# One chunk projected ahead of the gate's loop, row splits in two buffers, one late set of scatters, projections without loops

## The chip, the cores and the metric

One core of a Trainium2 chip runs one whole decoder layer as one program. The metric is the time of one execution on the device in microseconds (us).

## The reference

The input is x (4 x 1024 tokens of 512 floats) and a context (4 x 2048 tokens). Everything is float32; the kernel gets that precision on TensorE by splitting each operand into a rounded high part and the rest, and by adding three products (hi·hi, hi·lo, lo·hi).

```
x = x + self_attention(norm(x))            # causal, 16 heads of 32; q, k, v, out: y @ W.T
x = x + cross_attention(norm(x), context)  # 16 heads; Q, K, V: y @ W; out @ W_o + b_o
h = norm(x)
scores = h @ gate_W + gate_b               # 4 experts
top two experts of each token, softmax over the two scores
expert e: norm(relu(norm(h @ W1 + b1) * g1 + be1) @ W2 + b2) * g2 + be2
x = x + h + sum over the two of weight * expert(h)
```

## The kernel before, in words

The program is a row of stages with a barrier of all engines between them: constants, the projection of x to q, k and v (`project`, called as "qkv1"), the self attention, a "bridge" (output projection, norm, cross queries), the projection of the context ("kv2", `project` again, with weights that the bridge has split), the cross attention, `finish`, and `experts`. Each engine has its own list of instructions, in an order written out by hand, and waits on semaphores. SP's queue issues the loads and stores, strictly in its order, and a wait there holds everything behind it.

`project` works in chunks of 512 tokens (4 tiles of 128). A tile is turned on TensorE (L359), split by ScalarE (high, L327) and VectorE (low, L282); the next chunk's tiles are turned between the 12 products of this one (L376, L379). Each product is 12 matmuls. For qkv1 a block of its own, `load_weights` (L75), comes first: it turns and splits each of the three 512 x 512 matrices whole, in one PSUM buffer. Then a second block starts the norm (L261 to L276) and the products. The first three batches are passes of a hardware loop (L195), the last is written out.

`finish` goes over 8 chunks of 512 tokens. For chunk c it loads the attention rows (`a_in`, two buffers, L1345), splits them (`a_hi`, `a_lo`, one buffer each, L1453 and L1516), projects them tile by tile (`project_tile`, 14 matmuls, L1634 to L1637) and adds them to the tokens in `x_in` (three buffers, L1522). Then come the moments (L1495), a root on GpSimd (L1389), the normalising on ScalarE (L1439 and, for the output's base, L1443), stores of both (L1372, L1374), the turn (L1643) and split (L1469, L1600), the gate's scores (L1663), their turn (L1671) and the gate on VectorE (L1532 to L1553). Eight tiles (chunks 0 and 1) are projected before the loop; in turn c of the loop chunk c+2 is projected between the turns of chunk c. A chunk's tokens may be loaded once the base that lay in their buffer is stored:

```python
def load(c):
    after(sp, base_stored[c % 3], 16 * (c // 3))
```

In turn c SP issues, in this order: attention rows of c+3, `xn` of c, base of c, tokens of c+3, and in every second turn a matrix of the experts' first weights (`raw`, two buffers, L1355), which ScalarE and VectorE split (L1448, L1512).

The gate puts each token into the list of its two experts, in DRAM, by indirect DMAs of GpSimd, here called scatters: 16 for a chunk, 128 entries of 8 bytes each (L1397). Chunks 0 to 5 are scattered in `finish`, each set in the turn behind its gate and behind that turn's root. The last `LATE` = 2 chunks' 32 scatters are the first work of GpSimd in `experts` (L1821); SP loads the lists when all have landed (L1790), GpSimd gathers the tokens (L1798), TensorE turns them (L1849), they are split (L1900, L1965), and the first product begins (L1839). Meanwhile the second weights are loaded and split (L1895, L1989), in the lists of ScalarE and VectorE ahead of the first tokens.

## Time and profile before

| | |
|---|---|
| median of 3 runs | 4392.72 us (4384.69 to 4401.05) |
| profiled execution | 4395.31 us, its span 4393.6 us |
| TensorE busy | 4007.7 us, 91% of the span |
| VectorE, GpSimd, ScalarE busy | 62%, 59%, 48% |
| first product | 50.43 us |
| finish begins, experts' first scatter, first product | 3563.33, 3828.40, 3894.78 us |

A share over the whole span says little about stages that differ; the rows below are of the stages that the change touches. "Idle before" in a row is the time in which that engine did nothing ahead of the instruction, and the arrow names what ended it.

### The profile page before, as it was taken

What the parts mean: (1) busy time and instruction counts of PE and PEld (TensorE: products, weight loads), DVE (VectorE), ACT (ScalarE), POOL (GpSimd) and SP (SyncE); (2) the same over time, 40 slices, a digit from 0 to 9 for tenths busy, and PEclk for the clock granted to TensorE, in tenths of its full rate; (3) what the DMA queues carried; (4) which work ended last, traced back from release to release, by engine and by line L of the source; (5) the groups of instructions that cost most, each with busy time, mean ns of one, the idle gap of its engine ahead of it and who ended that gap; (6) DMA issues with size and microseconds to landing.
All of it is one profiled execution on the core that took longest, in us unless ns stands there. A gap on an engine that the chain in (4) does not pass through costs nothing. (4 is left out here: it accounts for less than half of the span.)

```text
span 4393.6 us, 60336 instructions
## 1 busy us (share of the span) xinstructions
PE 4007.7 (91%) x21522; PEld 2473.6 (56%) x21522; DVE 2715.0 (62%) x4942; ACT 2119.2 (48%) x3905; POOL 2592.9 (59%) x964
## 2 busy tenths in 40 slices
PE   6997999997989998999999999999999967459997
PEld 5884555554767886444444444444444435348885
DVE  4435777773543335777777777777777525337675
ACT  2112555554332110566666666666666634336665
POOL 0002455454000001799999999999999945548887
PEclk8996999998999997999999999999999978679998
DMA  4546544522545556022222222222222036644444
GB/s 144 181 158 143 115 95 101 115 51 92 189 172 167 174 177 169 17 59 59 59 57 59 59 59 59 59 59 59 59 59 59 6 139 125 126 82 78 84 81 63
DMA packets 270843, 424.34 MB, mean 97 GB/s; under 512 B 31562, under 2 KB 131914, under 8 KB 264395
## 3 DMA queue, kind: packets, MB, share of 16 engines
q1 hardware_dynamic: 246826, 381.84, 33.7%
q0 software_dynamic: 19776, 36.85, 5.0%
q8 instruction: 161, 2.64, 0.3%
q10 hardware_dynamic: 3968, 2.10, 0.2%
q14 instruction: 112, 0.91, 0.1%
HBM read 250.18 MB, written 170.52 MB: 96 GB/s over the span
## 5 line engine op out<-in xcount | busy, mean ns | idle before, releaser
L884 DVE TENSOR_REDUCE cross_neg_max<-cross_scores 128x1 f32<-128x512 f32 x2048 | 1265.7, 677 | 394.8 <-PE cross_scores L711 394.8
L668 POOL TENSOR_TENSOR cross_partial<-cross_partial,cross_probs 128x2048 f32<-128x2048 f32 x320 | 1465.6, 4580 | 67.3 <-ACT cross_probs L835 29.0
L835 ACT ACTIVATE cross_probs<-cross_shifted 128x512 f32<-128x512 f32 x2048 | 1074.4, 607 | 741.4 <-PE cross_shifted L723 706.5
L711 PE MATMUL cross_scores<-cross_k_stack,cross_q_stack 96*128 96x512 f32 x2048 | 876.8, 438 | 40.2 <-DVE cross_neg_max L884 27.2
L723 PE MATMUL cross_shifted<-cross_q_stack,cross_k_stack 98*128 98x512 f32 x2048 | 851.9, 420 | 11.6 <-ACT cross_probs L835 5.6
L723 PEld LDWEIGHTS cross_shifted<-cross_q_stack,cross_k_stack 98*128 98x128 f32 x2048 | 387.9, 190 | 382.6 <-issue 232.0
L711 PEld LDWEIGHTS cross_scores<-cross_k_stack,cross_q_stack 96*128 96x128 f32 x2048 | 395.8, 193 | 287.5 <-DVE cross_neg_max L884 224.1
L835 ACT ACTIVATE self_probs<-self_shifted 128x512 f32<-128x512 f32 (+3 forms) x768 | 358.5, 491 | 351.6 <-PE self_shifted L726 268.0
L884 DVE TENSOR_REDUCE self_neg_max<-self_scores 128x1 f32<-128x512 f32 (+3 forms) x768 | 388.4, 548 | 189.4 <-PE self_scores L711 97.0
L739 PE MATMUL cross_out<-cross_probs,cross_v 128*32 128x512 f32 x4096 | 492.7, 598 | 0.0
L711 PE MATMUL self_scores<-self_k_stack,self_q_stack 96*128 96x512 f32 (+3 forms) x768 | 308.4, 423 | 22.4 <-DMA self_k_stack<-k_hi 10.0
L723 PE MATMUL self_shifted<-self_q_stack,self_k_stack 98*128 98x512 f32 (+3 forms) x768 | 299.5, 409 | 12.2 <-issue 11.4
L668 POOL TENSOR_TENSOR self_partial<-self_partial,self_probs 128x2048 f32<-128x2048 f32 (+1 forms) x64 | 239.5, 3743 | 52.9 <-ACT self_probs L835 48.2
L650 POOL MEMSET cross_neg_max<- 128x128 f32 x1 | 0.2, 209 | 438.8 <-POOLq L2025 438.8
L739 PEld LDWEIGHTS cross_out<-cross_probs,cross_v 128*32 128x32 f32 x4096 | 107.0, 109 | 230.1 <-issue 178.6
L723 PEld LDWEIGHTS self_shifted<-self_q_stack,self_k_stack 98*128 98x128 f32 x768 | 151.5, 198 | 112.1 <-issue 79.8
L666 POOL TENSOR_TENSOR cross_partial<-cross_probs 128x2048 f32<-128x2048 f32 x32 | 146.6, 4582 | 110.3 <-ACT cross_probs L835 110.2
L711 PEld LDWEIGHTS self_scores<-self_k_stack,self_q_stack 96*128 96x128 f32 x768 | 159.5, 208 | 50.0 <-DVE self_neg_max L884 30.1
L904 DVE RECIPROCAL cross_inv<-cross_sum_sb 128x64 f32<-128x64 f32 x256 | 137.2, 540 | 67.4 <-ACT cross_sum_sb L821 67.4
L674 POOL TENSOR_TENSOR self_mixed<-self_out_sb,self_inv 128x512 f32<-128x512 f32 x32 | 40.9, 1277 | 229.0 <-issue 229.0
L739 PE MATMUL self_out<-self_probs,self_v 128*32 128x512 f32 (+3 forms) x1536 | 146.4, 499 | 0.0
L904 DVE RECIPROCAL self_inv<-self_sum_sb 128x128 f32<-128x128 f32 x128 | 117.4, 933 | 45.9 <-ACT self_sum_sb L821 45.9
(273 smaller groups left out, 6101.3 us busy)
## 6 DMA issues: line engine op xcount, KB each, us to landing
cross_k_stack<-k_hi SPq DMA_DIRECT2D x30, 1024.0 KB, 19.3
kv_x_in<-in_ctx SPq DMA_DIRECT2D x16, 1024.0 KB, 5.5
k_hi<-kv_out_hi SPq DMA_DIRECT2D x64, 256.0 KB, 2.6
k_lo<-kv_out_lo SPq DMA_DIRECT2D x64, 256.0 KB, 3.3
v<-kv_out_n SPq DMA_DIRECT2D x64, 256.0 KB, 2.3
cross_v<-v SPq DMA_DIRECT2D x32, 512.0 KB, 25.8
self_q_stack<-q_hi SPq DMA_DIRECT2D x30, 512.0 KB, 6.9
self_k_stack<-k_hi SPq DMA_DIRECT2D x30, 512.0 KB, 15.2
```

What stands on the lines that cost most here:

```text
L650: pool.memset(neg_max[:, :, :, :], 3.0e38).then_inc(filled.sem, 1)
L666: nc.gpsimd.tensor_tensor(total, probs[:, (e - 1) % PB, :, :], own, ALU.add).then_inc(pool_added.sem, 1)
L668: nc.gpsimd.tensor_tensor(total, total, own, ALU.add).then_inc(pool_added.sem, 1)
L674: nc.gpsimd.tensor_tensor(mixed[:, q % 2], out_sb[:, q % 2], inv[:, :], ALU.mult).then_inc(scaled.sem, 1)
L711: mm = nc.tensor.matmul(scores[at][:, 0:width], q_st[0:96, w, h, q0:q0 + P], k_st[0:96, w, h, half * WIDE:half * WIDE + width], start=True ...
L723: mm = nc.tensor.matmul(shifted[n % SHIFTED][:, f:], k_st[0:98, w, h, kt * P:(kt + 1) * P], q_st[0:98, w, h, qb * QB + f:(qb + 1) * QB], s ...
L739: mm = nc.tensor.matmul(out_ps[32 * h:32 * h + 32, f:], v_sb[:, w, kt, 32 * h:32 * h + 32], probs[:, e % NE % PB, h, f:], start=kt == 0, s ...
L835: nc.scalar.activation(probs[:, e % NE % PB, h, f:], shifted[n % SHIFTED][:, f:], ACT.Exp).then_inc(exped.sem, 1)
L884: nc.vector.tensor_reduce(neg_max[:, q % 2, column(a), half:half + 1], scores[n % (SLOTS * ROUNDS) % AHEAD][:, 0:width], AX.X, ALU.max, ne ...
L904: nc.vector.reciprocal(inv[:, cols], sum_sb[:, cols]).then_inc(inverted.sem, 1)
```

## The change

`load_weights` and the hardware loops go. `project` is one block with every chunk written out. With matrices to turn (qkv1), matrix 0 is turned in four quarters through the same two PSUM buffers as the tokens, behind the moments of chunk 0 in VectorE's list; the eight quarters of matrices 1 and 2 are turned one in front of each of the first eight products, and chunk 1's tiles in front of the last four. All three raw matrices have a buffer. kv2 has nothing to turn.

```diff
+            if turning:
+                load_matrix(0)
+            load(0)
+            for m in range(1, turning):
+                load_matrix(m)
+            load(1)
...
+        def turn_at(u, n):
+            if u == 0 and turning:
+                return ("matrix", n // KT + 1, n % KT) if n < KT * (turning - 1) else ("tokens", 1, n - KT * (turning - 1))
+            if n % (NOUT // TPC) == 0 and u + 1 < LAST:
+                return "tokens", u + 1, n // (NOUT // TPC)
+            return None
...
+            def turn_matrix(m, k):
+                if k == 0:
+                    pe.wait_ge(raw_loaded[m], 16)
+                after(pe, lo_ready, matrix_at(m) + k - 1)
+                for q in range(KT):
+                    mm = nc.tensor.transpose(turned[k % 2][:, q, :], raw[:, m, q, k * P:(k + 1) * P], ident[:, :])
+                mm.then_inc(turned_ready, 1)
...
             if norm:                                    # VectorE
+                variance(0)
+            for k in range(KT if turning else 0):
+                matrix_low(0, k)
+            if norm:
+                normalise(0)
+            for t in range(TPC):
+                tokens_low(0, t)
+            if norm:
+                variance(1)
+                normalise(1)
```

In `finish` the loop's turn 0 projects chunk 1, turn 1 projects chunk 2 ahead of everything and chunk 3 in between, and from turn 2 it is chunk c+2 as before. The row splits have two buffers, so that a split waits for the projection of two chunks back; it moves to the head of the turn on ScalarE and into its middle on VectorE. `raw` has one buffer, and the matrices are loaded in turns 1, 3 and 5.

```diff
-LATE = 2
+LATE = 1
...
-        a_hi = sb("a_hi", [P, KT, CH], F32R)
-        a_lo = sb("a_lo", [P, KT, CH], F32R)
+        a_hi = sb("a_hi", [P, 2, KT, CH], F32R)
+        a_lo = sb("a_lo", [P, 2, KT, CH], F32R)
-        raw = sb("raw", [P, 2, KT, D])
+        raw = sb("raw", [P, KT, D])
...
+        def ahead(c):
+            return c + 2 if c else 1
...
             def load_weight(m):
-                if m == 1:
-                    sp.wait_ge(ow_lo_ready, 1)
-                after(sp, w_lo_ready, m - 1)
+                sp.wait_ge(ow_lo_ready, 1)
+                after(sp, w_lo_ready, m)
...
-                if c % 2 == 0 and c // 2 + 1 < EXPERTS:
+                if c % 2 and c // 2 + 1 < EXPERTS:
                     load_weight(c // 2 + 1)
...
             for c in range(CHUNKS):                     # ScalarE
+                if c and c + 3 < CHUNKS:
+                    attention_high(c + 3)
                 after(act, scored, c)
...
+                if c == 0:
+                    attention_high(3)
                 if c % 2 == 0:
                     weight_high(c // 2)
-                if c + 3 < CHUNKS:
-                    attention_high(c + 3)
...
             for c in range(CHUNKS):                     # VectorE
+                if c == 1:
+                    for t in range(TPC):
+                        add_projection(2, t)
                 for t in range(TPC):
...
-                    if t == 0 and c + 1 < CHUNKS:
+                    if t == 0 and c and c + 1 < CHUNKS:
                         variance(c + 1)
-                    if t and c + 2 < CHUNKS:
-                        add_projection(c + 2, t - 1)
+                    if t == 1 and c and c + 3 < CHUNKS:
+                        attention_low(c + 3)
+                    if t and ahead(c) < CHUNKS:
+                        add_projection(ahead(c), t - 1)
...
+                if c == 0:
+                    variance(1)
+                    scales(1)
+                    attention_low(3)
                 gate(c)
...
-            for t in range(2 * TPC):                    # TensorE
-                project_tile(t // TPC, t % TPC)
+            for t in range(TPC):
+                project_tile(0, t)
             for c in range(CHUNKS):
+                if c == 1:
+                    for t in range(TPC):
+                        project_tile(2, t)
                 for t in range(TPC):
                     turn_tile(c, t)
-                    if t and c + 2 < CHUNKS:
-                        project_tile(c + 2, t - 1)
+                    if t and ahead(c) < CHUNKS:
+                        project_tile(ahead(c), t - 1)
```

## Rows read from the trace of the kernel before

**Rows 1.** Stretch, its us; busy PE, PEld, DVE, ACT, POOL; clock, DMA, GB/s

```profile
0.00:50.43 50.43, 15.57 (x69) 13.59 (x69) 18.95 (x33) 9.30 (x8) 4.01 (x16) 0.69 0.36 125
...
3563.33:3828.40 265.07, 176.75 (x738) 130.44 (x738) 126.01 (x344) 94.56 (x127) 118.33 (x121) 0.78 0.64 147
3828.40:3894.78 66.38, 2.23 (x9) 1.44 (x9) 10.39 (x5) 8.66 (x5) 39.19 (x36) 0.50 0.74 136
1316.40:1711.60 395.20, 388.43 (x1792) 316.60 (x1792) 130.00 (x192) 73.26 (x128) 0.00 (x0) 0.98 0.55 167
```

**Rows 2.** Timeline of the first 60 us: start, us, instruction, idle before

```profile
22.86 2.29 DVE L133 TENSOR_TENSOR qkv_w_lo<-qkv_w_turned,qkv_w_hi 128x2048 fp32r<-128x2048 f32 x1 [5.81 <-ACT qkv_w_hi L125]
...
33.86 2.47 DVE L261 BATCH_NORM_STATS2 qkv_stats<-qkv_x_in 128x6 f32<-128x512 f32 x4 [0.60 <-PEq L79]
...
38.23 1.92 DVE L276 TENSOR_SCALAR qkv_x_n<-qkv_x_in,qkv_mean_var,qkv_rstd 128x512 f32<-128x512 f32 x4 [1.17 <-POOL qkv_rstd L246]
...
44.06 0.69 DVE L282 TENSOR_TENSOR qkv_xt_lo<-qkv_turned,qkv_xt_hi 128x512 fp32r<-128x512 f32 x1 [0.16 <-ACT qkv_xt_hi L327]
...
50.43 2.06 PE L376 MATMUL qkv_acc<-qkv_xt_hi,qkv_w_hi 128*128 128x512 f32 x4
```

**Rows 3.** DMA issues of the first 60 us: KB each, us to landing

```profile
qkv_w_raw<-in_L_attn_k_heads SPq DMA_DIRECT2D x1, 1024.0 KB, 7.6
...
qkv_x_in<-in_x SPq DMA_DIRECT2D x3, 1024.0 KB, 11.9
```

**Rows 4.** TensorE at the seam between two passes of the first projection

```profile
121.87 0.60 PE L359 MATMUL qkv_turned<-ident,qkv_x_n 128*128 128x128 f32 x4
122.22 1.21 PE L376 MATMUL qkv_acc<-qkv_xt_hi,qkv_w_hi 128*128 128x512 f32 x4
```

**Rows 5.** GpSimd's timeline, first scatters of some sets of sixteen

```profile
3656.42 2.98 POOL L1397 DMA_INDIRECT lists<-finish_pairs,finish_place  x1 [9.48 <-DVE finish_place L1557]
...
3770.32 2.82 POOL L1397 DMA_INDIRECT lists<-finish_pairs,finish_place  x1 [11.62 <-DVE finish_place L1557]
...
3793.81 1.03 POOL L1397 DMA_INDIRECT lists<-finish_pairs,finish_place  x1 [0.64 <-DVE finish_place L1557]
...
3828.40 0.96 POOL L1821 DMA_INDIRECT lists<-lists_pairs,lists_place  x1 [13.10 <-POOLq L2025]
```

**Rows 6.** Timeline of finish: row split, normalising, tokens of chunk 7

```profile
3592.77 2.29 DVE L1516 TENSOR_TENSOR finish_a_lo<-finish_a_in,finish_a_hi 128x2048 fp32r<-128x2048 f32 x1 [1.31 <-ACT finish_a_hi L1453]
...
3599.49 2.93 ACT L1439 ACTIVATE finish_x_n<-finish_x_in,finish_shift,finish_rstd 128x512 f32<-128x512 f32 x4 [6.76 <-DVE finish_rstd_one L1508]
...
3763.45 0.69 DVE L1522 TENSOR_TENSOR finish_x_in<-finish_acc,finish_x_in 128x512 f32<-128x512 f32 x1 [10.48 <-DMA finish_x_in<-x]
```

**Rows 7.** Who waited for whom in finish on TensorE: us, times, longest

```profile
PE finish_acc L1634 <- DVE finish_a_lo L1516: 29.8, 7, 4.5
```

**Rows 8.** DMA issues of short stretches of finish, by the us from issue to landing

```profile
out<-finish_x_in SPq DMA_DIRECT2D x1, 1024.0 KB, 4.2
...
out<-finish_x_in SPq DMA_DIRECT2D x1, 1024.0 KB, 20.7
...
out<-finish_x_in SPq DMA_DIRECT2D x1, 1024.0 KB, 33.6
...
finish_a_in<-attn SPq DMA_DIRECT2D x1, 1024.0 KB, 17.6
...
finish_a_in<-attn SPq DMA_DIRECT2D x1, 1024.0 KB, 28.1
```

**Rows 9.** The sync queue's timeline, load of chunk 5's rows

```profile
3641.48 0.36 SPq L1345 DMA_DIRECT2D finish_a_in<-attn  x1
```

**Rows 10.** Timeline from the last weight to the experts' first product

```profile
3872.23 1.91 ACT L1895 ACTIVATE experts_w_hi<-experts_t 128x2048 fp32r<-128x2048 f32 x1 [15.58 <-DMA experts_t<-in_L_ffn_W]
3892.35 1.02 ACT L1900 ACTIVATE experts_yt_hi<-experts_x_turned 128x1024 fp32r<-128x1024 f32 x1 [18.21 <-PE experts_x_turned L1849]
...
3894.78 2.07 PE L1839 MATMUL experts_acc<-experts_w_hi,experts_yt_hi 128*128 x4 [2.46 <-DVE experts_yt_lo L1965]
```

More of the change, by code:

```diff
@@ new lines, in project, with after @@
+        loaded = [sem(f"loaded{u}") for u in range(2)]
+        step = sem("dve_step")
+        rooted = sem("rooted")
+        normed = sem("normed")
+        turned_ready = sem("turned_ready")
+        hi_ready = sem("hi_ready")
+        lo_ready = sem("lo_ready")
+        acc_ready = sem("acc_ready")
+        out_hi_ready = sem("out_hi_ready")
+        out_lo_ready = sem("out_lo_ready")
+        stored = [sem(f"stored{s}") for s in range(4)]
+        block = ctx.enter_context(nc.Block())
+        def after(eng, semaphore, value):
+            if value > 0:
+                eng.wait_ge(semaphore, value)
@@ L216, in chunk, with load_matrix @@
+            def load_matrix(m):
+                sp.dma_start(raw[:, m], weights[m][0].rearrange("(k p) n -> p k n", p=P)).then_inc(raw_loaded[m], 16)
+            if turning:
[4 more added lines that the diff above has]
+            load(1)
+            for u in range(LAST):
                 for n in range(NOUT):
                     kind, g, s = outs[n // 4][0], n % 4, n % 4
-                    if n == 0 and (more or u + 2 < chunks):
-                        load(it, u + 2)
@@ L232, in _ @@
             for s in range(4):
-                stored[s].give_credit(sp)
-            passes(sp, chunk)
-            for s in range(4):
-                sp.wait_ge(stored[s].sem, stored[s].at(BATCH, 0))
+                sp.wait_ge(stored[s], 16 * stores[s] * LAST)
         @block.gpsimd
@@ L241, in _ @@
                 return
[L243 to L250 removed]
+            for u in range(LAST):
+                pool.wait_ge(step, 3 * u + 3)
+                after(pool, normed, TPC * u)
+                nc.gpsimd.tensor_tensor(rstd[:, :], var_eps[:, :], neg_half[:, :], ALU.pow).then_inc(rooted, 1)
@@ L310, in _ @@
-            if norm:
-                variance(0, 0)
-                normalise(0, 0)
-            for t in range(TPC):
-                split_lo(0, 0, t)
-            if norm:
-                variance(0, 1)
-                normalise(0, 1)
-            passes(dve, chunk)
+                    dve.wait_ge(acc_ready, u * NOUT + n + 1)
+                    after(dve, stored[s], 16 * stores_before(s, u, n))
+                    nc.vector.tensor_copy(out_n[:, s], acc[s][:, :]).then_inc(out_lo_ready, 1)
@@ L364, in chunk @@
+            for u in range(LAST):
+                pe.wait_ge(lo_ready, chunk_at(u) + TPC)
                 for n in range(NOUT):
                     w, g, s = n // 4, n % 4, n % 4
-                    if n in TURN and (more or u + 1 < chunks):
-                        turn(it, u + 1, TURN[n])
-                    pe.wait_ge(out_lo_ready.sem, out_lo_ready.at(it, u * NOUT + n - 3))
+                    turn = turn_at(u, n)
+                    if turn and turn[0] == "matrix":
+                        turn_matrix(*turn[1:])
+                    elif turn:
+                        turn_tokens(*turn[1:])
+                    if u == 0 and n and g == 0 and turning:
+                        pe.wait_ge(lo_ready, matrix_at(w) + KT)
+                    after(pe, out_lo_ready, u * NOUT + n - 3)
@@ L1299, in finish @@
         added = sem("added")
[L1300 removed]
+        raw_loaded = sem("raw_loaded")
         w_hi_ready = sem("w_hi_ready")
```

310 lines of the change are left out of this document (115 added, 195 removed).

## The prediction

> **What bounds the kernel now.** I read the busy time by stage first, because the change touches three stages that run one after the other: the first projection, the stage behind the cross attention ("finish") and the start of the experts. Each ends at a barrier of all engines, so what a stage gains or loses moves everything behind it. [rows 1] says which engine a stage could still use: before 50.43 us TensorE is busy for 15.57 us, in the context's projection (code that the first one shares) for 388 of 395, in finish for 177 of 265, and in the 66 us before the experts' first product for 2 us. So the places to look at are the first 50 us, the loop of finish, and the way from the last lists to the first product.
>
> **The first 50 us.** A block turns and splits the three matrices one whole matrix at a time, the engines in turn: VectorE splits for 2.29 us and sits idle 5.81 for the other two [rows 2]. Only behind it does the norm of the first tokens begin, at 33.86 us [rows 2], though those tokens were there at about 16.6 us (issue 4.7, landing 11.9 later [rows 3]). The first product then waits for the norm of the *second* chunk, to 50.43 us.
>
> New order. The loads are queued as matrix 0, tokens 0, matrices 1 and 2, tokens 1. The second megabyte landed at 11.8 (issue 4.20, 7.6 later), the fourth at 16.6 [rows 3]: 2.4 us each, so matrix 0 is there at about 9.3 and the fifth at about 19. VectorE takes the moments of chunk 0 at 11.9 to 15.1 us (3.2 us: 38.23 less the root's wait of 1.17, less 33.86 [rows 2]), splits quarters 0 and 1 of matrix 0 (0.65 each), waits for quarters 2 and 3 to be turned (1.0) and split by ScalarE (0.6), and is done at about 19.2. Normalising begins there instead of at 38.23, 19.0 earlier, and the four tiles are split 6.5 us later, at 25.7 (the last began at 44.06 and took 0.69 [rows 2]). Now the product waits only for one turned quarter of matrix 1: start 26.6 instead of 50.43, 23.8 us earlier. Eight more groups of four transposes than before stand among chunk 0's products, at 0.35 us each (the 122.22 behind the 121.87 [rows 4]): 2.9 us. VectorE norms chunk 1 at 25.7 to 31.9 and then catches up with the quarters of matrix 1; by its list it has split the last at 40.6, and TensorE wants it at about 40.8. So **20.9 us gained**, bounds 15 (VectorE late by a moments pass of 3.2, and a cold clock) and 24 (the turns fill waits).
>
> **Straight code instead of loops.** The seam between two passes falls at 121.87, and the next product begins 0.35 us behind it, just as behind any other turn [rows 4]. In the projection of the context TensorE is busy 388.4 of 395.2 us [rows 1]. There is nothing to win in either, and the fourth pass is straight already. I take 0; more code to fetch has no row before, so bounds of -2 (the register moves ahead of stores) and +4 (1% of 395).
>
> **Finish: the first chunks.** Chunk c means: project its attention rows (four tiles, 3.2 us each), norm, turn, score, gate. Before, eight tiles are projected ahead of the loop. Now only chunk 0's are, then chunk 1's in turn 0. The moments of chunk 0 no longer stand behind a row split of 2.29 us and its wait of 1.31 [rows 6], so normalising starts at 3596 instead of 3599.49. But then things stand in a row: the second row split on VectorE holds the turned tiles (TensorE waits 3603.8 to 3606.8), chunk 1 is projected to 3620.6, and its moments and root (4.4, from 3595.1 to 3599.49) and normalising (5.9, two rows of 2.93) stand ahead of chunk 0's scores on ScalarE: TensorE waits 12 us, to 3632.6. The split for chunk 3 (1.9 + 2.3), gate 0 (4.0), four cold tiles of chunk 2 and three of chunk 3 follow. I get the first scatter at 3662.5, where it was at 3656.4 [rows 5]: **6 us lost**, bounds 3 and 10. What overlapped projection with norm is gone here.
>
> **Finish: a chunk in the middle.** Before, the split of the next rows (2.29) sits between the gate and the first tile [rows 6], and TensorE waited 29.8 us for it in seven times [rows 7]. With two buffers it is out of the way: by VectorE's list a chunk could take 22.7 us instead of 26.3. GpSimd can't follow: sixteen scatters and a root are 21.7 to 25.6 us from one first scatter to the next (3770.32 to 3793.81 is 23.5 [rows 5]). So at best 23.7 per chunk.
>
> **The loads under the scatters.** While GpSimd scatters, DMA is slow: a megabyte stored in front of the scatters took 4.2 us to land, under them 20.7 as second and 33.6 as fifth of one burst; a load took 17.6 as second and 28.1 as third [rows 8]. The sync queue waits in order, so this decides. Two edits make it worse. (1) The row buffer for the expert weights is single: load_weight(1) now waits for the split of weight 0, which VectorE does in turn 1 behind the positions, at 3664.5. The load of chunk 5's rows is queued behind that wait; it was issued at 3641.48 [rows 9] and lands now as second under scatters, 3665.4 + 18 = 3683. (2) ScalarE wants these rows at the head of turn 2 (3671) instead of its end, before it splits a turned tile. Turn 2 is held by 12 us. Its out store lands between scatters, so chunk 6's rows come in time. Chunk 7's are loaded only when chunk 3's output has landed: normalised at about 3701, stored 3704, landed 20.7 later at 3724.6, then third in the burst behind tokens and a weight, 21 to 28 us: 3750. ScalarE wants them at 3730: **20 us held**. From there to the scatter of chunk 3 are 14.5 us: 3765, where it was at 3735.9. Chunk 4's follows 23.7 later, at 3788.7 (was 3770.32). Tokens of chunk 7 (VectorE waited for them until 3763.45 [rows 6]) come at about 3764 and are not late.
>
> **The late chunk.** From chunk 4's scatter to the end of the early ones were 3770.32 to 3815.3, and 13.1 more to the first late one (3828.40 less its idle 13.10 is 3815.3 [rows 5]). Now a third early set (about 21.7) stands in front of that gap: 58.1 + 21.7 = 79.8, so the experts' stage starts its scatters at 3868.5 instead of 3828.4. Behind it come 16 instead of 32: from there to the first product it was 66.4 us (3828.4 to 3894.78 [rows 10]); 22.2 go, and what lies behind the last scatter stays. So moving a set across the barrier by itself is worth nothing; it only turns the order. What is late next are the weights: ScalarE split the last at 3872.23, VectorE 2.3 later, 18 us ahead of the first tokens at 3892.35. By rows that chain is 49.6 from the first late scatter to the product, against 44.2 by the lists. With scatters over after 22 us the last load should be faster; I take 45. First product: 3913.5 against 3894.8, **18.7 us lost** in finish and behind.
>
> By the row on the second load under scatters, 17.6, this stands. The Trainium skill (DMA: Bandwidth & Descriptors, "Anatomy of one DMA") gives a DMA 2.0 us and its bytes at 436 GB/s, 4.4 us a megabyte; the trace agrees only where nothing scatters (4.2). By it the attention rows would be in time, and the sum would be that of the first rival below. That page, under "Queues, rings and completion order", also says that an engine takes turns between queues packet by packet, which would let bulk loads pass small writes; the 33.6 speaks against it.
>
> **Sum.** The profiled execution took 4395.31 us for a span of 4393.6; -20.9 + 0 + 18.7 = -2.2 gives 4393.1. It stood 2.6 above the median of the runs shown, so on that median it is 4390.5, say 4391.
>
> **Rivals.**
> A, GpSimd bounds finish. If loads land fast enough (gaps between sets, other timing), sets follow at 23.7 from 3662.5: chunk 4's at 3757, first late scatter at 3837, product at 3882, 12.5 earlier. Total -33: 4360. For it: 4.2 us landings without scatters. Against: GpSimd stood idle 11.62 us in front of 3770.32 [rows 5], in the end for tokens. Chance 0.19.
> B, only the tokens of chunk 7 bound, as before: chunk 4's set at 3770, +79.8 + 45 = 3895, nothing lost. Total -21: 4372. Chance 0.12.
> C, slower: the DMA queue never drains. It decides if chunk 5's rows land as the third did (28 instead of 18) and the whole turn is 10 later; chunk 6's then hold turn 3 by 3 more, chunk 7's issue waits 33.6 instead of 20.7 and lands after 28: chunk 3's set at 3791, 26 later than in my sum. Total +24: 4416. Chance 0.15.
> My forecast has 0.54, its own range 4380 to 4403.
>
> **How the numbers follow.** 0.5% is 22 us, about what a measurement of this kernel can tell. Faster than 4371: all of A, a third of B: 0.23. Slower than 4415: most of C and a bit of mine: 0.13. The rest, 0.64, is within. The range 4360 to 4413 leaves out half of A's lower side and half of C.
>
> **What would show it.** First product at 26 to 28 us, end of the first projection's products near 311 instead of 331.6. No difference in length of the context's projection. First scatter near 3642 on the new clock (20.9 less), VectorE and TensorE stopped in turn 2 and turn 4 with ScalarE waiting for finish_a_in, by about 12 and 20 us. A finish stage of about 305 us instead of 265, and 45 instead of 66 us from the experts' first scatter to the first product. I am wrong if ScalarE does not wait for its rows, if sets of scatters follow each other without gaps, or if the first product is behind 32 us.

## The result: 0.28% slower, and the profile after

The changed kernel takes **4407.84 us** (median of 8 runs, 4403.75 to 4410.21) against 4393.41 for the kernel before in the same comparison: ratio 1.0028, 95% interval 1.0019 to 1.0036. That is 14.4 us slower by the medians and 12.3 by the ratio. 4391 was forecast, and -2.2 us for the profiled execution; its span is 4404.8, 11.2 more than before. Four single executions in the experiments below were slow ones (5021 to 18762 us), and their medians and ratios leave these out.

Stretches of the changed kernel, in the columns of [rows 1]: first projection up to its first product, finish, the first late scatter to the experts' first product, the context's projection.

```profile
0.00:26.36 26.36, 8.61 (x37) 6.91 (x37) 11.01 (x23) 6.06 (x9) 3.02 (x15) 1.00 0.69 239
3547.41:3856.27 308.86, 171.93 (x738) 126.44 (x738) 125.53 (x344) 95.32 (x127) 129.39 (x137) 0.77 0.55 127
3856.27:3906.84 50.57, 2.23 (x8) 1.44 (x9) 10.39 (x5) 8.66 (x5) 21.67 (x20) 0.50 0.78 178
1297.00:1701.40 404.40, 390.60 (x1792) 316.27 (x1793) 130.00 (x192) 73.34 (x128) 7.34 (x3) 0.98 0.54 167
```

Against [rows 1]: the first product comes at 26.36 instead of 50.43; finish lasts 308.9 instead of 265.1 with TensorE busy for 172 of it, where it was 177; 50.6 instead of 66.4 follow, and the context's projection takes 404.4 where it took 403.4 over the same stretch (its first turned tile to the first cross score; the 395.2 of [rows 1] is a shorter one). The chain of the first 26 us, VectorE's timeline:

```profile
12.04 2.47 DVE L195 BATCH_NORM_STATS2 qkv_stats<-qkv_x_in 128x6 f32<-128x512 f32 x4 [12.04 <-DMA qkv_x_in<-in_x]
...
18.42 0.69 DVE L218 TENSOR_TENSOR qkv_w_lo<-qkv_turned,qkv_w_hi 128x512 fp32r<-128x512 f32 x1 [0.16 <-ACT qkv_w_hi L267]
19.03 1.91 DVE L211 TENSOR_SCALAR qkv_x_n<-qkv_x_in,qkv_mean_var,qkv_rstd 128x512 f32<-128x512 f32 x4
...
24.85 0.69 DVE L223 TENSOR_TENSOR qkv_xt_lo<-qkv_turned,qkv_xt_hi 128x512 fp32r<-128x512 f32 x1 [0.16 <-ACT qkv_xt_hi L273]
```

The tokens are there at 12.04, normalising starts at 19.03 (forecast 19.2), the last tile is split at 25.5 (25.7). The last product of this projection begins at 310.6, against 330.5 before.

GpSimd's scatters in finish; the bracket is idle time and what ended it. They answer to [rows 5]:

```profile
3647.10 2.98 POOL L1353 DMA_INDIRECT lists<-finish_pairs,finish_place  x1 [7.09 <-DVE finish_place L1513]
...
3677.57 1.03 POOL L1353 DMA_INDIRECT lists<-finish_pairs,finish_place  x1 [7.03 <-DVE finish_place L1513]
...
3712.55 2.82 POOL L1353 DMA_INDIRECT lists<-finish_pairs,finish_place  x1 [7.39 <-DVE finish_place L1513]
...
3740.38 1.03 POOL L1353 DMA_INDIRECT lists<-finish_pairs,finish_place  x1 [3.46 <-DVE finish_place L1513]
...
3770.56 2.82 POOL L1353 DMA_INDIRECT lists<-finish_pairs,finish_place  x1 [9.09 <-DVE finish_place L1513]
...
3794.09 1.03 POOL L1353 DMA_INDIRECT lists<-finish_pairs,finish_place  x1 [0.64 <-issue]
...
3819.68 2.76 POOL L1353 DMA_INDIRECT lists<-finish_pairs,finish_place  x1 [5.58 <-DVE finish_place L1513]
...
3856.27 0.96 POOL L1787 DMA_INDIRECT lists<-lists_pairs,lists_place  x1 [14.83 <-POOLq L1991]
...
3876.21 2.96 POOL L1787 DMA_INDIRECT lists<-lists_pairs,lists_place  x1 [0.30 <-issue]
...
3898.33 1.00 POOL L1764 DMA_INDIRECT experts_x_rows<-xn,experts_entries  x1 [19.16 <-DMA experts_entries<-lists]
```

These are the first scatters of the seven sets of finish, the first and the last late one, and the gather that waits for the lists, 19.16 us. The first set starts 99.7 us into finish where it was 93.1; steps of 30.5 and 35.0 us follow. Why the early sets are slow shows on ScalarE, whose row splits for chunks 5, 6 and 7 are these:

```profile
3663.30 1.91 ACT L1409 ACTIVATE finish_a_hi<-finish_a_in 128x2048 fp32r<-128x2048 f32 x1 [8.48 <-DMA finish_a_in<-attn]
...
3697.91 1.91 ACT L1409 ACTIVATE finish_a_hi<-finish_a_in 128x2048 fp32r<-128x2048 f32 x1 [12.30 <-issue]
...
3726.12 1.91 ACT L1409 ACTIVATE finish_a_hi<-finish_a_in 128x2048 fp32r<-128x2048 f32 x1 [5.81 <-DMA finish_a_in<-attn]
```

and in the sync queue, first its issues and then two of its longest waits in finish (us in all, times, longest):

```profile
3649.07 0.37 SPq L1311 DMA_DIRECT2D finish_raw<-in_L_ffn_W  x1
3649.49 0.51 SPq L1302 DMA_DIRECT2D finish_a_in<-attn  x1
...
3652.67 0.38 SPq L1330 DMA_DIRECT2D out<-finish_x_in  x1
...
3679.54 0.51 SPq L1302 DMA_DIRECT2D finish_a_in<-attn  x1
```

```profile
SPq L1306 <- DMA out<-finish_x_in: 80.4, 5, 26.1
SPq L1296 <- DVE experts_w_lo L1470: 58.7, 3, 27.3
```

The load of chunk 5's rows went out 78.2 us into finish before (3641.48 [rows 9]); now it goes out at 102.1 (3649.49), behind a weight that waited for VectorE's split (L1296, a wait that is new). Chunk 5's rows land as ScalarE has waited 8.48 us, chunk 7's 5.81. Chunk 6's split comes 12.30 late, and for this one the profile names no releaser. Its rows were issued only at 3679.54, since the store of chunk 2's output, issued at 3652.67, held the queue for 26.1 us, the longest wait of L1306; and its buffer was free from 3688.2, when TensorE had done with chunk 4. So the rows are the likely cause, not a shown one. The wait of TensorE for row splits [rows 7] is gone, as the second buffer promises.

| us | before | after | forecast |
|---|---|---|---|
| first projection, to the first self score | 341.7 | 321.3 | -20.9 |
| from there to the start of finish | 3221.6 | 3226.1 | 0 |
| finish | 265.1 | 308.9 | +40.1 |
| first late scatter to first product | 66.4 | 50.5 | -21.4 |
| the rest | 498.8 | 498.0 | 0 |

-20.4 + 4.5 + 43.8 - 15.9 - 0.8 = +11.2. No line of the forecast is far off, but four of the five misses have one sign: +0.5, +4.5, +3.7, +5.5 and -0.8.

### The profile page after: what moved, and what is told of

It reads as the page before. It is cut to its first block and busy times, and to the rows that moved or that the text cites. A ratio compares the mean times of both kernels' runs of the same rounds, so it can differ in the third digit from the quotient of the medians.

```text
span 4404.8 us, 58985 instructions
## 1 busy us (share of the span) xinstructions
PE 3999.5 (91%) x21522; PEld 2464.0 (56%) x21522; DVE 2714.0 (62%) x4951; ACT 2121.6 (48%) x3914; POOL 2588.6 (59%) x964
## 5 line engine op out<-in xcount | busy, mean ns | idle before, releaser
L676 PE MATMUL cross_shifted<-cross_q_stack,cross_k_stack 98*128 98x512 f32 x2048 | 851.1, 420 | 13.6 <-ACT cross_probs L788 5.6
L664 PEld LDWEIGHTS cross_scores<-cross_k_stack,cross_q_stack 96*128 96x128 f32 x2048 | 395.2, 193 | 287.3 <-DVE cross_neg_max L837 224.5
L1353 POOL DMA_INDIRECT lists<-finish_pairs,finish_place x112 | 117.0, 1044 | 72.3 <-DVE finish_place L1513 39.7
L1873 ACT ACTIVATE experts_t<-experts_t,experts_neg_mean,experts_rstd 128x512 f32<-128x512 f32 x140 | 106.6, 809 | 79.5 <-DVE experts_neg_mean L1950 68.7
```

Of the source, the lines that this page charges most:

```text
L664: mm = nc.tensor.matmul(scores[at][:, 0:width], q_st[0:96, w, h, q0:q0 + P], k_st[0:96, w, h, half * WIDE:half * WIDE + width], start=True ...
L676: mm = nc.tensor.matmul(shifted[n % SHIFTED][:, f:], k_st[0:98, w, h, kt * P:(kt + 1) * P], q_st[0:98, w, h, qb * QB + f:(qb + 1) * QB], s ...
L1353: pool.indirect_dma_start(lists, bass.IndirectOffsetOnAxis(to[:, t, e:e + 1], 0), entry[:, t, e, :], None).then_inc(listed, 16)
L1873: nc.scalar.activation(dst[:, t], dst[:, t], ACT.Identity, scale=rstd[:, n, t:t + 1], bias=neg_mean[:, n, t:t + 1]).then_inc(ready, 1)
```

## Experiments

All numbers in one table first. "Finish" is from its start to the first late scatter, "behind" from there to the experts' first product, both from the profile; ratios are timed against the kernel before on the same chip. late4 was timed in two executions only, the second profile of before in one.

| kernel | ratio, 95% | median | finish | behind |
|---|---|---|---|---|
| before / second profile | 1 | 4391 to 4394 (4389 once) | 265.1 / 262.9 | 66.4 / 64.8 |
| after | 1.0028 (1.0019-1.0036) | 4407.8 | 308.9 | 50.5 |
| proj_only | 0.9968 (0.9956-0.9980) | 4378.7 | 266.4 | 62.6 |
| proj_again | 0.9965 (0.9953-0.9977) | 4376.3 | 263.5 | 64.0 |
| late2 | 1.0007 (0.9998-1.0016) | 4396.4 | 286.7 | 62.8 |
| late4 | 1.0053 (1.0035-1.0070) | 4417.3 | 267.1 | 101.6 |
| rows_first | 1.0013 (1.0003-1.0022) | 4400.1 | 307.3 | 48.2 |
| split_behind | 0.9993 (0.9985-1.0002) | 4390.8 | 293.4 | 48.1 |
| cols_act | 1.0034 (1.0021-1.0047) | 4402.5 | 301.9 | 47.9 |
| reads_first | 1.0015 (1.0006-1.0023) | 4401.2 | 304.8 | 46.6 |
| eight_ahead | 0.9972 (0.9961-0.9983) | 4382.8 | 283.6 | 51.1 |
| eight_late2 | 0.9966 (0.9953-0.9979) | 4371.2 | 259.2 | 64.1 |
| eight_late2_rows | 0.9962 (0.9948-0.9975) | 4374.2 | 260.7 | 62.2 |
| eight_late2_behind | 0.9951 (0.9938-0.9964) | 4364.5 | 252.6 | 67.6 |
| best_again | 0.9954 (0.9940-0.9967) | 4370.2 | 254.4 | 63.6 |
| behind_late1 | 0.9960 (0.9946-0.9974) | 4369.3 | 273.3 | 47.4 |
| behind_reads1 | 0.9954 (0.9941-0.9967) | 4372.8 | 283.8 | 45.4 |

The theory: the projection is the gain, finish the loss, by three edits (the order of the first chunks, the rows asked for early and issued late, the single late chunk). The rivals: the straight code costs time everywhere, or one of the three edits does it alone. Medians of different chips are compared below only beside the ratios.

**proj_only**, the kernel before with the new `project` in place of the old one and of `load_weights`, finish untouched.

> The kernel before with the new projection alone (both projections); finish and its two late chunks as before. Theory (finish carries the whole loss): first product at 26 us, finish as long as before (265 us) and 66 us from the first late scatter to the first product, so about 4393 - 20 + 2 to 4 of drift = 4375 to 4378. Rival (the straight code itself costs time all through the kernel): over 4385. Rival (the projection gains 20 and nothing else of the change matters in a bad way but an earlier finish collides): finish longer than 270 us.

4378.7, and 4376.3 in a second comparison: 14 to 15 us faster (0.32 and 0.35%). Finish and what is behind stay as they were. The change's loss lies in finish.

**before_again**, a second profile of the kernel before.

> The kernel before once more, for a second profile of it. In all ten profiles with the new projection the stages between the first projection and finish (self attention to the end of the cross attention, from the first self score to finish's first product) took 3234.5 to 3242.2 us; the one profile of before has 3234.6. Theory (this is scatter between executions): the second profile of before lies anywhere from 3234 to 3242. Rival (the new projection makes later stages slower by 3 to 4 us): 3235 again or less.

3229.7 us from the first self score to finish's first product, less than any of the sixteen profiles with the new projection (3234.6 to 3242.8, middle 3238.7); the first profile of before has 3234.6, as much as the lowest of them. That speaks against mere scatter: it looks as if some 6 us of the 20.4 that the projection gains are given back in stages whose code is the same or, in the context's projection, does the same work. By the means it is 3.1 us in the self attention, 0.6 in the bridge, 1.4 in the context's projection and 1.4 in the cross attention, but two profiles of before, 4.9 us apart, are too few to place it or to be sure of it. TensorE's busy time over that stretch is 3066 to 3069 us in before and after. This stays open.

**late2**, two late chunks in the changed kernel.

```diff
-LATE = 1
+LATE = 2
```

> The changed kernel with two late chunks of scatters again. Theory (the late chunk added a set of 21.7 us in finish and gave back only 15.9, since something other than the lists ends last behind it): finish 287 us, 66 us to the first product, 6 us less than the changed kernel: 4402. Rival (moving a set over the barrier is neutral, as forecast): 4408. Rival (the third set was the loss): under 4390.

9 us by the ratios (11.5 between the medians) come back, more than the 6 expected. What ends finish is another engine now. VectorE's last table entry and the first late scatter of late2:

```profile
3828.63 0.20 DVE L1536 TENSOR_TENSOR experts_table<-finish_expert_no,finish_first_step 128x35 int32<-128x35 f32 x1
```

```profile
3830.70 0.96 POOL L1787 DMA_INDIRECT lists<-lists_pairs,lists_place  x1 [23.44 <-POOLq L1991]
```

2 us apart: VectorE's count bounds finish, GpSimd has stood still for 23.44. In the changed kernel VectorE's last table entry is this:

```profile
3832.72 0.20 DVE L1536 TENSOR_TENSOR experts_table<-finish_expert_no,finish_first_step 128x35 int32<-128x35 f32 x1
```

Finish ends 23.5 us behind it and 36.6 behind the start of the seventh set (3819.68), 14.83 of them GpSimd's wait for its landings and the barrier: GpSimd bounds. Finish is 22.2 us longer than in late2, and 12.3 come back behind it. Of the 22.2, 3.4 are there already at chunk 4's set, where the two kernels still do the same, so the set itself costs nearer 19.

**eight_ahead**, the eight tiles ahead of the loop again.

```diff
-            return c + 2 if c else 1
+            return c + 2
...
-            for t in range(TPC):
-                project_tile(0, t)
+            for t in range(2 * TPC):
+                project_tile(t // TPC, t % TPC)
```

(and VectorE's and ScalarE's lists in the same way, all turns alike).

> The changed kernel with eight tiles projected ahead of the loop again and uniform turns (no gating of the first chunk ahead); two split buffers and one late chunk stay. Theory (the prelude in a row cost 6.6 us, the attention rows the rest): first scatter 93 us after the start of finish instead of 99.7, ScalarE still waits for its rows, time 4402. Rival (the new order of the first chunks is the whole cause): finish 287 us, 4386. Rival (the first scatter is absorbed by later waits for rows): 4408, no change.

25.1 us between the medians (24.6 by the ratios), more than any reading expected. The first set and the seventh:

```profile
3631.51 2.98 POOL L1353 DMA_INDIRECT lists<-finish_pairs,finish_place  x1 [8.68 <-DVE finish_place L1511]
...
3798.30 2.75 POOL L1353 DMA_INDIRECT lists<-finish_pairs,finish_place  x1 [7.80 <-DVE finish_place L1511]
```

Finish starts at 3550.7 here, so the first set is 80.8 us into it: 18.9 earlier than in the changed kernel and 12.3 earlier than before. The 6.6 of the comparison with before was the difference of two large things: a second buffer for the split rows, with the split in its new place, brings 12.3, the first chunk gated ahead costs 18.9. (Against the second profile of before, whose first set is 90.9 us in, it is 10.1; and where the split stands at the end of the turn again, in the four profiles below that have it so with eight tiles ahead, the first set is at 82.7 to 84.1.) Finish as a whole is 25.3 us shorter.

**rows_first**, the weight's load behind the next attention rows.

```diff
-                if c % 2 and c // 2 + 1 < EXPERTS:
-                    load_weight(c // 2 + 1)
...
                 if c + 3 < CHUNKS:
                     load_attention(c + 3)
+                if c and c % 2 == 0:
+                    load_weight(c // 2)
```

> The changed kernel with the expert weight's load queued behind the next attention rows instead of ahead of them (one load later in the queue, in turns 2, 4 and 6). Theory (the wait for the single weight buffer holds the attention rows): chunk 5's rows are issued 8 us earlier and chunk 7's are one place further ahead in the burst, ScalarE's waits of 8.5, 12.3 and 5.8 us shrink to under half in sum, finish 10 to 15 us shorter: 4394 to 4398. Rival (the DMA queues are slow under scatters whatever stands first): under 3 us of change, 4405 to 4411.

ScalarE's row splits of the same three chunks:

```profile
3650.14 1.90 ACT L1409 ACTIVATE finish_a_hi<-finish_a_in 128x2048 fp32r<-128x2048 f32 x1
...
3689.72 1.91 ACT L1409 ACTIVATE finish_a_hi<-finish_a_in 128x2048 fp32r<-128x2048 f32 x1 [13.61 <-DMA finish_a_in<-attn]
...
3712.14 1.90 ACT L1409 ACTIVATE finish_a_hi<-finish_a_in 128x2048 fp32r<-128x2048 f32 x1
```

Chunk 5's no longer waits at all, as the theory has it, but chunk 6's now waits 13.61: 26.6 us of waits became 13.6. The time is 7.8 us less by the medians and 6.6 by the ratios (0.15%), with intervals that overlap, where 10 to 14 were expected. And little of it is the theory's: finish is 1.6 us shorter instead of 10 to 15, the stretch behind it 2.3, and 4.5 us of the profile's 8.5 lie in the stages ahead of finish, which this edit does not touch. The wait for the single weight buffer is real, but taken away by itself it mostly passes to the next chunk.

**split_behind**, the row split at the end of the turn, into two buffers.

```diff
-                if c and c + 3 < CHUNKS:
-                    attention_high(c + 3)
                 after(act, scored, c)
...
                 if c % 2 == 0:
                     weight_high(c // 2)
+                if c and c + 3 < CHUNKS:
+                    attention_high(c + 3)
```

(and on VectorE from behind the second tile into the gate).

> The changed kernel (gated ahead, one late chunk, weight ahead of rows in SyncE's queue) with the row split back at the end of the turn (ScalarE) and in the gate (VectorE). Theory (the head of the turn asks for the rows too early): no wait of ScalarE for attention rows over 3 us in turns 2 to 4, 7 to 10 us shorter, 4398 to 4401. Rival (the rows are late for the end of the turn too, since their issue stands behind the weight's wait): waits of 5 us or more stay, 4404 to 4408.

17 us between the medians (15.4 by the ratios, 15.5 in finish), twice what was expected: the second largest cost in the changed kernel. With eight tiles ahead and two late chunks the same move brings only 6.6 in finish (eight_late2_behind below), so the costs of the edits do not simply add. ScalarE's row splits, none with a wait over 1.8 us, and the second, third and fourth set:

```profile
3655.91 1.90 ACT L1409 ACTIVATE finish_a_hi<-finish_a_in 128x2048 fp32r<-128x2048 f32 x1
...
3684.61 1.89 ACT L1409 ACTIVATE finish_a_hi<-finish_a_in 128x2048 fp32r<-128x2048 f32 x1
...
3709.75 1.90 ACT L1409 ACTIVATE finish_a_hi<-finish_a_in 128x2048 fp32r<-128x2048 f32 x1
```

```profile
3676.76 1.04 POOL L1353 DMA_INDIRECT lists<-finish_pairs,finish_place  x1 [1.90 <-DVE finish_place L1515]
...
3703.69 2.82 POOL L1353 DMA_INDIRECT lists<-finish_pairs,finish_place  x1 [4.14 <-DVE finish_place L1515]
...
3730.76 1.03 POOL L1353 DMA_INDIRECT lists<-finish_pairs,finish_place  x1 [3.27 <-DVE finish_place L1515]
```

The rows were not late in themselves: they are issued at 3652.28, still behind the weight, and are there by the end of the turn. Only the head of the turn, where ScalarE has four turned tiles behind them, was too early. The pace is 26.9 us; the 23.7 that the forecast held possible is not reached even here, GpSimd idles 2 to 4 us in front of a set for VectorE's places.

**cols_act** and **reads_first**: the experts' two loads in 4-byte elements (`cols`, 8 KB each) on ScalarE's queue, then also the first four list reads ahead of SyncE's waits for the weights' splits.

```diff
-                sp.dma_start(cols[:, k], ...
+                act.dma_start(cols[:, k], ...
...
+            sp.wait_ge(listed, 16 * LATE * TPC * EXPERTS)
+            for s in range(FIRST_LISTS):
+                read(s)
             sp.wait_ge(w2_lo_ready, 2)
             load_rows(2)
             sp.wait_ge(w2_lo_ready, 3)
             load_rows(3)
+            for s in range(FIRST_LISTS, STEPS):
+                read(s)
```

> The changed kernel (gated ahead, one late chunk) with the experts' two loads in 4-byte elements issued by ScalarE's queue at the head of the stage instead of SyncE's. Theory (SyncE's queue, 17 us in issuing these two, holds the reads of the lists): the first gather's entries land 8 us earlier, 42 to 43 us from the first late scatter to the first product instead of 50.5, 4400. Rival (the scatters' own landing or the weights end last): 48 us or more, 4406 to 4408. Rival (ScalarE, held in issuing, splits the first weight later): slower than 4410.

> The changed kernel with the 4-byte loads on ScalarE's queue, and the reads of the first four lists moved in SyncE's queue ahead of its waits for the splits of the second and third weight. Theory (behind a single late chunk the reads are held by SyncE's queue, not by the scatters): they are issued about 5 us behind the last scatter, as with two late chunks, and the first product comes 8 us earlier, 40 us from the first late scatter, 4395. Rival (the scatters' landing holds them): 47 us as in the run with the loads moved alone, 4403.

The sync queue behind the barrier, changed kernel first, then late2 and reads_first:

```profile
3865.86 16.91 SPq L1743 DMA_DIRECT2D experts_cols<-in_L_ffn_be  x1
...
3889.19 1.88 SPq L1733 DMA_DIRECT2D experts_rows<-in_L_ffn_be  x4
3893.73 5.58 SPq L1756 DMA_DIRECT2D experts_entries<-lists  x7
```

```profile
3864.36 4.31 SPq L1733 DMA_DIRECT2D experts_rows<-in_L_ffn_be  x4
3881.52 17.57 SPq L1756 DMA_DIRECT2D experts_entries<-lists  x18
```

```profile
3870.30 0.38 SPq L1736 DMA_DIRECT2D experts_t<-in_L_ffn_W  x1
3883.28 1.91 SPq L1749 DMA_DIRECT2D experts_entries<-lists  x4
```

With two late chunks the queue is free at 3868.7 and waits for the last scatter (issued 3876.4), so the reads go out 5 us behind it (10 in the kernel before, whose last scatter stands at 3872.73). With one, the scatters are out at 3876.2 and the queue comes free at 3891.1: the reads go 17.5 us behind the last scatter. It is issuing that fills the queue up to there, with no gap from 3855.6 on, and 16.91 us of it are one load of 8 KB. With the two small loads gone (cols_act), SyncE waits for the weights' splits in its place, 10.1 us in two waits, and the reads go out only 3.3 us sooner after the first late scatter. The order is as the theory has it, its size not: behind finish it is 2.6 us less with the loads moved and 1.3 more with the reads first, 46.6 instead of the 40 expected, and the first of these is no more than what kernels without this edit differ by (47.4 to 51.1 in five profiles with one late chunk). In reads_first the reads go out 9.4 us behind the last scatter, with nothing in their queue but the wait for the scatters. The gather then starts 5.7 us sooner than in cols_act, but its tokens reach TensorE 6.7 us after it instead of 3.4. Timed, cols_act is no faster than the changed kernel by its ratio, reads_first by 0.13%, with intervals that touch. That SyncE's queue held the reads is shown; that it was worth more than some 4 us is not.

**late4**, four late chunks.

> The changed kernel with four late chunks of scatters. Theory (with two or more late chunks VectorE's last count ends finish, so a set moved behind it costs its 20 to 22 us whole): finish as long as with two late chunks (286 us) or shorter by what the scatters took from the loads, 63 + 43 = 106 us from the first late scatter to the first product, 4438. Rival (the scatters in finish hold the loads so much that it gains from fewer): finish 270 us or less, under 4425.

The rival came true: finish 267.1, 19.6 shorter than with two. From finish's first product to the last projected tile late2 and late4 take the same 211 us; the difference comes behind it, in the turns of chunks 6 and 7, which have scatters beside them in one and none in the other. Chunk 7's root on GpSimd, which its normalising waits for, late2 and then late4:

```profile
3785.57 1.04 POOL L1345 TENSOR_TENSOR finish_rstd<-finish_var_eps,neg_half 128x4 f32<-128x4 f32 x1
```

```profile
3782.87 1.01 POOL L1345 TENSOR_TENSOR finish_rstd<-finish_var_eps,neg_half 128x4 f32<-128x4 f32 x1 [23.99 <-DVE finish_var_eps L1460]
```

In late2 the root stands right behind sixteen scatters on GpSimd's queue (no idle time before it), in late4 GpSimd had been idle for 23.99. From the normalising of chunk 6 to that of chunk 7 it is 23.5 us there and 17.5 here; and from there to the end of finish 43.8 against 30.4, in which ScalarE begins two of the four turned tiles 6.4 and 8.4 us late beside scatters, and none over 3.2 late without. So scatters in finish do cost more than GpSimd's time. But moved behind the barrier each set costs 19.4 us there (half of 101.6 less 62.8), and the sum is slower.

**eight_late2**, **eight_late2_rows**, **eight_late2_behind**: eight tiles ahead and two late chunks, then also the weight's load behind the rows, then also the split at the end of the turn.

> The changed kernel with eight tiles projected ahead and two late chunks: of the change to finish only the two split buffers, the split's new place in the turn and the single weight buffer are left. Theory (the order of the first chunks and the late chunk cost independently of each other, 24.5 and 11.5 us): 4372, that is 6 us less than the new projection alone, since two split buffers shorten the way to the first scatter by 12 us. Rival (the costs overlap, the two buffers bring nothing in the end, because the last chunk's own gating ends the stage): 4378 to 4384.

> As the run before (eight tiles ahead, two late chunks), and the weight's load queued behind the next attention rows. Theory (attention rows behind the weight's wait hold turns 1 and 3 by 13 us in sum; the order takes back what it did in the changed kernel, 5.7 us): 4366. Rival (rows then wait elsewhere, for the store and the burst): 4370 to 4374, the same within 2 us.

> As the run before, with the row split at the end of the turn (ScalarE) and inside the gate (VectorE), where the kernel before had it, but into two buffers. Theory (the head of the turn asks for the rows a third of a turn too early): ScalarE does not wait for attention rows at all, time 4362 to 4366. Rival (the split of 2.3 us stands again between the gate and the next turned tile, eight turns): 4372 to 4378.

eight_late2 fits the sum by its median (4371.2) but is by its ratio no better than the projection alone; the order of the loads adds nothing that can be told from it (rival right); the split at the end of the turn brings finish to 252.6, 12.5 us less than before (10.3 less than in before's second profile), and the time to 4364.5, as expected: ScalarE waits 1.8 us for rows in all.

**best_again** (eight_late2_behind once more), **proj_again**, and **behind_late1** (best_again with one late chunk), on one chip.

> The fastest kernel so far once more, beside the others on one chip: new projection, eight tiles ahead, two split buffers with the split at the end of the turn, rows ahead of the weight, two late chunks. Theory: ratio to before 0.993 to 0.996 as before (4364 on a before of 4389 to 4394).

> The kernel before with the new projection alone, once more, beside the fastest. Theory (the two split buffers bring 3 to 8 us once the split stands at the end of the turn): 4370 to 4379, slower than the fastest by 4 to 9 us. Rival (finish's changes bring nothing at all, the earlier difference lay between two chips): within 3 us of it.

> The fastest kernel with one late chunk instead of two and nothing else. Theory (GpSimd's seventh set ends finish, and SyncE's queue holds the reads of the lists behind the barrier): 8 to 12 us slower than the fastest on the same chip. Rival (one late chunk is neutral, as forecast, and the gap measured in the changed kernel came from its other waits): within 3 us of the fastest.

The fastest, again: 0.9954, 4370.2, some 20 us faster than before and 32 (by the ratios) to 38 (by the medians) faster than the changed kernel. The projection alone is 6 us behind it, with intervals that overlap, so it is likely but not shown that what is left of the change to finish is worth anything. And **one late chunk makes no difference that can be told here** (4369.3 against 4370.2, each ratio known to some 6 us either way): 18.9 us more in finish, 16.2 less behind. The theory that it costs 8 to 12 by itself is not borne out; the forecast's claim that it is worth nothing by itself stands where nothing else holds the turns. **behind_reads1**, the same kernel with the edits of reads_first, says the same.

> Eight tiles ahead, two split buffers with the split at the end of the turn, rows ahead of the weight, one late chunk, the 4-byte loads on ScalarE's queue and the first lists read early: the mildest surroundings for one late chunk. Theory (one late chunk adds a set of 22 us to a finish that GpSimd then bounds and gives back at most 20): 4364 to 4368, no better than the same with two late chunks (4364.5). Rival (with the reads freed, one late chunk pays): under 4360.

Its ratio is that of best_again, its median 4372.8 where 4364 to 4368 was expected. Its profile has one step of 33 us between two early sets, so its finish is 10.5 us longer than behind_late1's, and the stretch behind it is 2.0 us shorter.

## Why the prediction was wrong

Right: the new projection's first 26 us, step by step within half a microsecond; the first scatter (6.6 us later, 6 forecast); the new wait of SyncE for the single weight buffer; ScalarE waiting for its rows at the head of the turn (rows_first and split_behind show both causes at work); no gain from straight code. None of the three rivals came, though C's hold of turn 3 did, for another reason.

The sum missed by 13.4 us of profile. Most of it is the late chunk, in both halves of its term; the third miss lies in the stages between the first projection and finish.

- **From chunk 4's set to the first late scatter, 79.8 taken, 85.7 measured (5.9 us).** The forecast added one set of 21.7 us, the lowest of its own range (21.7 to 25.6), to the 58.1 of the profile before. That is about GpSimd's own time for a set (21.5 from 3793.81 to 3815.3 before) and leaves out that the set waits for VectorE's places. Chunk 6's set waited 5.58 us and came 25.6 behind chunk 5's, and the end of finish came 36.6 behind it where it was 34.6. All eight profiles with one late chunk agree: 5.0 to 7.9 us of waiting, 25.1 to 27.8 for the set, 84.4 to 87.4 for the whole.
- **Behind the late scatters, 45 taken, 50.5 measured (5.5 us).** The forecast had two paths, 44.2 by the lists and 49.6 by the weights, and took 45 because "the last load should be faster". It was: ScalarE split the last weight 35.6 us behind the first late scatter, before 43.8, and VectorE was done with it 10.7 us ahead of the product. (The 49.6 does not come out of its rows either; they give 48.0 to the end of VectorE's split.) So the weights did not end last, the lists did, and the step that failed is "what lies behind the last scatter stays". It was 22.1 us (3872.73 to 3894.78) and became 30.6 (3876.21 to 3906.84), because SyncE was still issuing other loads until 3891.1 and sent out the reads 17.5 us behind the last scatter instead of 10.0. Before, the queue was free at 3867.6, ahead of the last of 32 scatters. I had counted that queue's contents in finish and not here.

```profile
3872.73 0.95 POOL L1821 DMA_INDIRECT lists<-lists_pairs,lists_place  x1 [0.31 <-issue]
```

```profile
3891.86 1.91 ACT L1861 ACTIVATE experts_w_hi<-experts_t 128x2048 fp32r<-128x2048 f32 x1 [9.01 <-DMA experts_t<-in_L_ffn_W]
```

- **The stages between, 0 taken, +4.5 measured.** Against two profiles of before and sixteen with the new projection it is about 6. Its cause is not known, and it may in part be scatter. It would explain why the projection, 20.4 us where it acts, is worth 14 to 15 in the time.

Finish as a whole came out near the forecast, 308.9 for 305, partly by luck. The holds were placed in turns 2 and 4 (12 and 20 us); they came in turns 2, 3 and 4 (8.5, 12.3, 5.8). "Its out store lands between scatters, so chunk 6's rows come in time" failed: that store took 26.1 us. Chunk 3's set then stood 193.0 us into finish where 201.7 was forecast, and the step to chunk 4's was 30.2 instead of 23.7, so that chunk 4's set was only 2.2 us off, at 223.2 for 225.4. Nor was the 58.1 typical: in the profile before, chunk 4's set was late (207.0 us into finish) for the tokens of chunk 7, and in its second profile, with that set at 196.6, 66.3 us followed. That a late chunk is worth nothing by itself is right as far as behind_late1 can tell, but in the changed kernel the late chunk did not cost 21.7 and give 21.4: finish grew by 22.2 against late2 and 12.3 came back.

The price of 4.4 us a megabyte that the forecast quotes from the Trainium skill (DMA: Bandwidth & Descriptors, "Anatomy of one DMA") is given there for DMAs that GpSimd issues, while these loads are issued by SyncE; the sum did not use it.

The forecast's own range ended at 4403. The bounds that it gave its terms (+4 for more code, 49.6 behind the scatters, and 15 instead of 20.9 for the projection) come to 4405, close to the 4407.8 measured, though the last of them did not happen. I had added their middles.

## What to carry over

Ask of a stage behind a barrier what stands in the issuing queue ahead of the transfer you wait for, not only when the data is ready. An operand that is moved from the end of a turn to its head must have landed a turn's rest earlier; measured here, that cost 15 to 17 us in the changed kernel, and 7 in a milder one, although the second buffer it filled was free. When a piece of work is added to an engine's list, take the step from one such piece to the next, waits included, and not the engine's own time (21.7 taken, 25 to 28 measured). And an edit that comes out at 6 us may be 12 gained and 19 lost: cost its halves one by one, then one of them can be left out.

## What the runs showed of the hardware

- The straight code shows as traffic. DMA queues of the kernel before, then of the changed one: packets, MB, share:

```profile
q8 instruction: 161, 2.64, 0.3%
```

```profile
q8 instruction: 173, 2.83, 0.3%
```

Twelve packets more, 0.19 MB, 5 of them in the first projection and 7 in the context's, none in between. The Trainium skill (Runtime: NRT & Kernel Launch, "Instruction fetch mechanics") says that an engine streams its code in blocks of 16 KiB over a DMA queue of its own, which fits, and that a taken branch whose target is not at hand stalls for such a fetch. By that the loops removed should have cost something; the trace shows no gain from them, 403.4 and 400.7 us with the loop in the context's projection, 402.0 to 404.5 without.
- Beside scatters, ScalarE began instructions 6.4 and 8.4 us late with no present work named as releaser: its splits of chunk 7 in late2, then in late4, where nothing scattered. Why is not settled.

```profile
3801.69 0.60 ACT L1427 ACTIVATE finish_xt_hi<-finish_turned 128x512 fp32r<-128x512 f32 x1 [6.41 <-issue]
3810.73 1.08 ACT L1427 ACTIVATE finish_xt_hi<-finish_turned 128x512 fp32r<-128x512 f32 x2 [8.44 <-DMA attn<-cross_mixed]
```

```profile
3798.61 0.60 ACT L1427 ACTIVATE finish_xt_hi<-finish_turned 128x512 fp32r<-128x512 f32 x1 [3.13 <-PE finish_turned L1606]
3799.46 0.60 ACT L1427 ACTIVATE finish_xt_hi<-finish_turned 128x512 fp32r<-128x512 f32 x1 [0.26 <-PE finish_turned L1606]
```

- Issuing the second of the two loads in 4-byte elements (8 KB) held SyncE for 13.1 to 19.8 us in the profiles where SyncE had issued 5 MB of loads just ahead of it (17.5 before, 16.9 after), and ScalarE for 3.19 in cols_act, where ScalarE issued it at the head of the stage:

```profile
3849.88 3.19 ACTq L1855 DMA_DIRECT2D experts_cols<-in_L_ffn_be  x1
```

- The reads of the lists, which wait for all late scatters to land, went out 3.8 us (late4) to 11.0 us (eight_late2_behind) behind the issue of the last scatter in the kernels where SyncE's queue held nothing else back; 5.2 in late2, 10.0 in before, 9.4 in reads_first. What sets it within that range is not settled.
